# First routed tile's rows loaded ahead of the tables, four key/value projections moved into the feed-forward

## What is computed

```
x = x + linear_attention(layernorm(x), ctx, ctx)               # q softmax over 8, k softmax over 64
x = x + ffn_low_rank(layernorm(x), U1, V1, U2, V2, b1, b2)     # rank 128, inner 1376
x = x + attention(layernorm(x), ctx, Wq, Wk, Wv, Wo)           # keys/values of [ctx, latents], 16 heads of 96, 4 kv heads
x = x + moe(layernorm(x), gate_w, bias, Wg, Wu, Wd, Sg, Su, Sd) # 16 experts, top 4, and one shared expert
```

## Time and profile before

| | us |
|---|---|
| median of 3 runs | 708.01 |
| lowest, highest | 707.88, 709.03 |
| the profiled execution | 709.7 |
| its span, first to last instruction | 707.6 |
| mean granted TensorE clock | 0.987 of full |

### The profile page before, as it was taken

The page is one execution under the profiler, slowest core; times in us unless marked ns, Lnnn a source line. Parts: engine busy times, 40 slices in busy tenths (PEclk is TensorE's granted clock), DMA queues, the critical chain, the costliest instruction groups (busy, mean ns, idle before and its releaser), DMA issues.

```text
span 707.6 us, 9751 instructions
## 1 busy us (share of the span) xinstructions
PE 679.5 (96%) x2460; PEld 404.0 (57%) x2461; DVE 346.2 (49%) x838; ACT 193.3 (27%) x543; POOL 176.3 (25%) x226
## 2 busy tenths in 40 slices
PE   9999899999999999999999999996999999999992
PEld 7555343446777777777776785673444444444440
DVE  3998433544234446576665767454233333333331
ACT  4453322212244433323333242220111111111110
POOL 2354210101000000013513314255033332332342
PEclk9999999999999999999999999999899999999996
DMA  9999997133300110001104105312866757768544
GB/s 335 406 421 420 422 421 325 45 125 114 134 0 1 33 58 0 1 16 46 60 2 149 59 2 175 123 75 63 280 172 114 179 103 181 183 130 235 91 74 59
DMA packets 60403, 103.19 MB, mean 146 GB/s; under 512 B 7200, under 2 KB 32544, under 8 KB 59712
## 3 DMA queue, kind: packets, MB, share of 16 engines
q1 hardware_dynamic: 30608, 73.61, 27.8%
q0 software_dynamic: 8816, 18.00, 12.8%
q10 hardware_dynamic: 20944, 11.15, 5.4%
HBM read 46.60 MB, written 56.26 MB: 145 GB/s over the span
## 4 chain that ended last, share of the span: by engine, by line
PE 79%; issue 8%; DVE 4%; DMA 3%; SPq 2%; ACT 1%; POOL 1%; POOLq 0%; DVEq 0%; ACTq 0%
PE ps L1196 48%; PE ps L1377 9%; PE ps L1346 4%; PE ps L1184 4%; PE ps L1362 4%; PE ps L1295 3%; PE ps L1296 3%; PE ps L1305 3%; DVE rq L964 2%; DMA r<-in_ctx 2%; DMA out<-rq,sidx 1%; PE ps L1315 1%; SPq L412 1%; SPq L418 1%; PE ps L1237 1%
## 5 line engine op out<-in xcount | busy, mean ns | idle before, releaser
L1196 PE MATMUL ps<-kv,rq 128*128 x432 | 195.3, 601 | 6.0 <-SPq L520 5.4
L1196 PEld LDWEIGHTS ps<-kv,rq 128*128 128x128 f32 x432 | 79.8, 193 | 94.9 <-issue 94.7
L1196 PE MATMUL ps<-zT,r 128*128 128x256 f32 (+1 forms) x552 | 132.5, 395 | 0.9 <-ACT kv L697 0.9
L1196 PEld LDWEIGHTS ps<-zT,r 128*128 128x128 f32 x552 | 103.4, 190 | 24.5 <-issue 11.2
L1377 PE MATMUL ps<-r 128*128 128x512 f32 x192 | 85.1, 593 | 0.0
L624 POOL DMA_INDIRECT out<-rq,sidx x36 | 56.7, 1574 | 111.9 <-DMA out<-rq,sidx 83.3
L551 POOL TENSOR_SCALAR ve<-mv 128x1 f32<-128x1 f32 x32 | 7.2, 224 | 289.5 <-DVE mv L933 289.5
L735 ACT ACTIVATE r<-ps,snm 128x128 f32<-128x128 f32 x128 | 45.3, 366 | 82.4 <-DVE snm L1029 78.9
L1123 DVE TENSOR_TENSOR rq<-ps,rq 128x256 f32<-128x256 f32 x36 | 15.3, 424 | 104.3 <-ACT rq L787 104.3
L1377 PEld LDWEIGHTS ps<-r 128*128 128x128 f32 x192 | 35.2, 190 | 38.3 <-issue 38.3
L787 ACT ACTIVATE rq<-ps 128x256 f32<-128x256 f32 x36 | 13.8, 384 | 125.0 <-PE ps L1196 115.1
(11 more groups left out here) (176 smaller groups left out, 844.9 us busy)
## 6 DMA issues: line engine op xcount, KB each, us to landing
slot_rows<-rq SPq DMA_DIRECT2D x4, 8192.0 KB, 50.7
kv<-in_experts SPq DMA_DIRECT2D x54, 256.0 KB
rq<-slot_rows ACTq DMA_DIRECT2D x136, 64.0 KB
r<-in_Wq SPq DMA_DIRECT2D x1, 3072.0 KB, 21.2
r<-in_Wo SPq DMA_DIRECT2D x2, 1536.0 KB, 6.4
r<-in_ctx SPq DMA_DIRECT2D x8, 256.0 KB, 8.3
xr<-in_x SPq DMA_DIRECT2D x8, 256.0 KB, 8.4
second_norm_rows<-zrow SPq DMA_DIRECT2D x8, 256.0 KB, 2.2
```

What stands on the lines that cost most here:

```text
L1196: mm = pe.matmul(out, lhs(k), rhs(k), start=(k == 0), stop=(k == n - 1))
```

## The change

1. Context units 12 and 13 leave the iterations of tiles 5 and 6 of the first attention (and the later ones move up one or two places). Unit 12 now stands in the first half of the feed-forward between `f_gu` of tile 1 and `f_z` of tile 0, unit 13 between the half's last two `f_z`.
2. Two latent `v` units (of tiles 0 and 1) leave the second attention's start and stand in the second half of the feed-forward, one between its last two `f_z`, one behind the last. The remaining units of the half are reordered, with the `ln_t` and `q` steps around them; in half 1 too, two `v` units now come ahead of the `k` units.
3. These four units use banks 7, 7, 7 and 2, with waits to suit: `f_in` of half 1 waits for the copy of unit 13, `f_out` of tile 5 for that of unit 14.
4. SP waits for the scattered rows first, loads block 0 with four DMAs of fixed address ahead of the tables, and afterwards only the second tile's block by `tab`.

```diff
-            lat_units.append([("k", t, h, 1) for t in range(3)] + [("v", j, 1) for j in range(4 * h, 4 * h + 4)])
+            lat_units.append([("v", j, 1) for j in range(4 * h, 4 * h + 2)] + [("k", t, h, 1) for t in range(3)]
+                             + [("v", j, 1) for j in range(4 * h + 2, 4 * h + 4)])
...
-            if j in (3, 5, 6):
+            if j == 3:
                 prog.append(unit())
...
+                if (h, c) == (0, 1):
+                    prog.append(unit())
                 if c:
                     prog.append(("f_z", h, c - 1))
...
+            prog.append(unit() if h == 0 else ("kv", lat_units[0][0]))
             prog += [("f_z", h, NF - 1), ("f_oz", h)]
+            if h == 1:
+                prog.append(("kv", lat_units[0][1]))
...
-        for i, u in enumerate(lat_units[0]):
+        for i, u in enumerate(lat_units[0][2:]):
...
-            if 2 <= i < 6:
+            if i >= 2:
                 prog.append(("ln_t", 2, 2 + i))
-            if i in (2, 4, 6):
-                prog.append(("q", 0, i // 2))
+            if i in (1, 3, 4):
+                prog.append(("q", 0, (i + 1) // 2 + i // 4))
+        prog.append(("ln_t", 2, 7))
...
+        def load_first_block(eng):
+
+            for b in range(4):
+                eng.dma_start(xrow[b * QD:(b + 1) * QD, 0, :].rearrange("p (a e) -> p a e", a=4),
+                              quads_d[0, b, :, :, :]).then_inc(s_gx[0], 16)
...
-            return ps[:, 6 + n % 2 if n < EARLY_KV else 7, :]
+            return ps[:, {12: 7, 13: 7, 14: 7, 15: 2}.get(n, 6 + n % 2 if n < EARLY_KV else 7), :]
...
+            for k in range(TOPK):
+                sp.wait_ge(s_zs[k], 16 * J)
+            load_first_block(sp)
             sp.wait_ge(s_tabl, 1)
             loads = sp.value_load(head[0:1, 2:3], min_val=TOPK, max_val=E)
-
             sp.wait_ge(s_tab, 1)
-            for k in range(TOPK):
-                sp.wait_ge(s_zs[k], 16 * J)
-            for i in range(2):
-                block_of = sp.value_load(tab[0:1, i:i + 1], min_val=0, max_val=P)
-                load_block(sp, block_of, i, s_gx[i])
+            load_block(sp, sp.value_load(tab[0:1, 1:2], min_val=0, max_val=P), 1, s_gx[1])
...
+                    if n in (12, 13) or n >= EARLY_KV:
+                        pe.wait_ge(s_prc, n)
+                    elif n == 14:
+                        pe.wait_ge(s_x2, 4)
+                    elif n == 15:
+                        pe.wait_ge(s_act, 2 * NF - 1)
...
                     else:
                         pe.wait_ge(s_ptc, 1)
+                        pe.wait_ge(s_prc, len(ctx_units))
```

10 lines of the change are left out of this document (6 added, 4 removed).

## The result

| | before | after |
|---|---|---|
| median of 20 runs each, same chip | 708.75 | 706.07 |
| lowest, highest | 707.79, 712.61 | 703.51, 708.79 |
| the profiled execution | 709.7 | 706.84 |
| its span | 707.6 | 704.7 |

The account below looks back on a forecast made before the run. PE was taken to bound the kernel, so closing its pauses shortens the end. The terms 0 - 1.8 - 1.5 - 3.0 = -6.3 us took the median from 708.0 to 701.7, range 697.6 to 705.4.

Parts of the forecast that it names:

- Context units, 0: First attention and feed-forward: moving units 12 and 13 sums to 0, between 0.6 us lost and 0.5 won.
- Latent units, -1.8: End of the feed-forward's second half: two `v` units close PE's pauses of 0.76 and 0.68, 1.8 us won.
- First tile's start, -1.5: Gap before the routed tiles: with the first block loaded early, the first tile starts at 494.5 instead of 496.01.
- Clock, -3.0: First routed tiles: a pause of 3.9 us, shorter than 4.6, keeps the full clock and wins 3.0 us.
- The rival that took over this case: First routed tiles: the clock's 3.0 us is not won, giving 704.7; chance 0.25.
- A tile loop that starts earlier ends earlier by as much.: Routed tiles: PE sets the pace at 5.37 us per tile, so an earlier start moves the end and tail equally.
- Number 2: Gap before the routed tiles: DVE's wait goes or shrinks with SP's moved steps, PE goes straight on, 697.8; chance 0.15.
- Number 3: Gap before the routed tiles: the change does nothing there, feed-forward's 1.8 or less is left, 706.2 to 708.5; chance 0.08.
- Number 4: Gap before the routed tiles: SP's early loads start the slow steps, first tile at 500, 710.2; chance 0.05.

Follow-up runs that it names:

- e6: The changed kernel, unedited, run again on another chip: 707.33 us, ratio 0.9952 to the kernel before.
- e8: The changed kernel with SP's loads of the first block back behind the tables, same chip as e6: 707.83 us, ratio 0.9973 to the kernel before.
- e17: The changed kernel, unedited, on a further chip: 707.19 us, ratio 0.9960 to the kernel before.
- e18: The changed kernel with SP's first block load back behind the tables, same chip as e17: 708.48 us, ratio 0.9986 to the kernel before.
- e7: The changed kernel with POOL's last eight scatters of token ids waiting for the turn of the first block: 711.57 us, ratio 1.0023 to the kernel before.
- e14: The changed kernel with 16 matmuls of zeros in PE's pause ahead of the first routed tile: 704.51 us, ratio 0.9925 to the kernel before.
- e1: The changed kernel with SP's block loads as before, so the four moved units alone: 700.15 us, ratio 0.9970 to the kernel before.
- e9: The changed kernel with only the last tile's four id scatters waiting for the first block's turn: 705.57 us, ratio 1.0046 to the kernel before.
- e11: The kernel of e9 with SP's load of the fourth expert also held until the first output addition landed: 705.96 us, ratio 1.0050 to the kernel before.

## Why the prediction was wrong

**Starting point.** 708.01 was a median of three; over 20 runs it is 708.75. By the ratio the gain is 3.1 against the 6.3 forecast, half of it. From 708.01 the same gain would give 704.9, just inside the range; that would not have made the sum right.

**Context units, 0.** Right in the whole and in each step: `f_in` at 72.49 for the 72.6 said, the reciprocal of tile 7 free of PE, the first half's pauses closed, 0.49 at the second `f_in` for the 0.6 said. At the second `f_in` the kernel was 0.17 early.

**Latent units, -1.8.** Right: 1.9 earlier at the shared expert, and 2.1 (chip B), 1.9 (C) and 1.0 (F, interval to 0) by the ratios of the kernel that has the units alone.

**First tile's start, -1.5.** Right in mechanism and near in size: 1.9 in the profile, 1.1 and 2.2 between e6 and e8, e17 and e18. The sum let the add shift only with PE, from 492.44 to some 490.6; it came at 489.87, 0.5 behind the last scatter of POOL's run where it had been 2.0 behind. The run, without which e7 has no hold, had moved up by 1.05.

**Clock, -3.0.** This is the step that failed first. It took a pause of 3.9 to be safe because the one fall it had had come 4.6 behind PE's stop; over nine profiles it comes 2.1 to 4.7 behind. The pause was 3.5, and the clock fell 1.2 after the restart; 1.3 of 3.0 was won in the passes. The rival that took over this case gave 704.7, inside the range, and it was right that the clock falls, though it booked none of the 1.3. But e14 adds what neither had: even with the clock kept, the time is gone one tile later, because rows of the third tile are late. The 3.0 was read as PE's busy time and booked as time of the end.

**"A tile loop that starts earlier ends earlier by as much."** This is the second step that failed; without its loss the measured 706.07 would be 703.9, inside the range. Said of a loop whose tiles are PE-bound at 5.37, it left out the only other chain in it, addition to buffer to scaling, and the load that now starts ahead of the first addition. 2.2 of the 5.05 were lost (1.4 in the tiles, where DVE and PE wait behind the additions, and 0.8 in the tail, whose cause stays open). No rival covered it.

The sum with measured terms: -1.9 (units), -1.9 (start), -1.26 (clock), makes -5.05 at the loop's start, +1.4 (tiles), +0.8 (tail), makes -2.9, the difference of the spans.

**The rivals.** Number 2 (the hold goes with SP's moved steps) was wrong as to its cause: POOL's scatters, not SP's steps. It was right that without the hold PE goes straight on (e7, and all of chips B and D but e1 with its 0.83). The cause that I could not name in the prediction stood in a row quoted there: POOL's scatters ending at 490.4. Number 3 (nothing won at the gap, 706.2 to 708.5) is close to the 706.07 measured, but by luck: 3.1 were won at the gap and 2.2 lost behind it. Number 4 (slower, the early loads starting the slow steps) did not happen in any profile.

**Open.** Why chips differ in the hold; what lengthens the tail; what the changed kernel gives without it; how often the additions are slow in unprofiled runs, and so what holding the load would be worth.

## What to carry to other kernels

When a stage is to start earlier, list every queue that its first items share with the end of the last stage (here the fourth expert's load and the first output addition): their order is part of the timing and may flip. A cost that PE shows in busy time, such as a low clock, is worth only what the next engine's input lets through, so look up when the next tile's rows land before booking it. And where an engine stands for no reason that the profile names, look for what ends with the wait, and move that once to see.

## What the runs showed of the hardware

- On the chips with the hold (C, E, F, and the one called A), each profile with a run of twelve GpSimd scatters, 1.27 apart, has VectorE's add 6.3 to 7.2 late, let go 0.5 to 2.2 behind the run's end, ScalarE's copy 2.3 to 4.6 late, and SyncE's four loads drawn out from 1.8 to between 3.1 and 3.9; TensorE's own matmuls went on with gaps of 0.2 to 0.7. Moving eight scatters away ended it (e7). Two other chips showed none of it with such a run, and there the kernel before takes 701.8 and 702.3 against 708.8 to 710.7.
- The granted clock fell 2.1 to 4.7 behind TensorE's last matmul in nine profiles with a pause of 3.3 to 5.6 there (in `after` 1.2 after the restart), and stayed at 1.00 in the two kernels under the hold that filled the pause with zero matmuls.
- An output addition on the software queue beside an expert's load on a hardware queue still moved packets over 5 us behind its issue (e9); with the load held it was through within 5.2 (e11). In `after`, issued 0.6 behind the load's start, it moved its first packet over 4 us later, against 2 to 3 in the kernel before.
